# Half of the next tile's q projection moved ahead of the attention products on TensorE

## What is computed

```python
for i in range(6):
    x = attn_layer(shift_tokens(x), Wqkv[i], q_scale[i], k_scale[i], Wo[i]) + x
    x = ffn_layer(shift_tokens(x), ln_g[i], ln_b[i], W1[i], b1[i], W2[i], b2[i]) + x

def attn_layer(x, Wqkv, qs, ksc, Wo):      # 16 heads of 64
    q, k, v = split(x @ Wqkv)
    q, k = l2norm(q) * qs, l2norm(k) * ksc
    q, k = rotated(q), rotated(k)           # rotary tables with a scale
    # windows of 32 tokens: each sees itself and the window before, masked
    attn = softmax(where(mask, -inf, q @ k.T * 8))
    return (attn @ v) @ Wo
```

## Time and profile before

| | before |
|---|---|
| median of 3 runs | 3400.34 us (3400.24 to 3401.74) |
| the profiled execution's own time | 3401.79 us |
| its span, first to last instruction | 3400.0 us |
| mean granted TensorE clock, share of full speed | 0.993 |
| busy, TensorE matmuls | 3276.1 us (96%) |
| busy, TensorE weight loads | 2159.4 us (64%) |
| busy, VectorE | 2734.4 us (80%) |
| busy, ScalarE | 2226.2 us (65%) |
| busy, GpSimd | 2560.1 us (75%) |
| DMA | 52.53 MB, mean 15 GB/s |

### The profile page before, as it was taken

The page is one execution under the profiler, slowest core; times in us unless marked ns, Lnnn a source line. Parts: engine busy times, 40 slices in busy tenths (PEclk is TensorE's granted clock), DMA queues, the critical chain, the costliest instruction groups (busy, mean ns, idle before and its releaser), DMA issues. The chain is left out here.

```text
span 3400.0 us, 101399 instructions
## 1 busy us (share of the span) xinstructions
PE 3276.1 (96%) x42193; PEld 2159.4 (64%) x42193; DVE 2734.4 (80%) x3698; ACT 2226.2 (65%) x4397; POOL 2560.1 (75%) x2957
## 2 busy tenths in 40 slices
PE   8999699999999999999999999999999999999996
PEld 5555366666666666666666666666666666666664
DVE  2333598888988888888888888888888888988884
ACT  2222367777677676776776767767767667676774
POOL 0000498888888888888888888888888888888882
PEclk9999899999999999999999999999999999999999
DMA  2000001000001000001000010000010000000000
GB/s 73 1 1 1 4 11 36 11 11 8 11 17 36 8 11 11 11 17 34 11 11 8 11 42 11 8 11 11 11 41 9 11 11 8 16 13 18 11 11 13
DMA packets 62284, 52.53 MB, mean 15 GB/s; under 512 B 11526, under 2 KB 59396, under 8 KB 61828
## 3 DMA queue, kind: packets, MB, share of 16 engines
q1 hardware_dynamic: 61828, 46.05, 5.3%
HBM read 43.93 MB, written 2.10 MB: 14 GB/s over the span
## 5 line engine op out<-in xcount | busy, mean ns | idle before, releaser
L477 POOL TENSOR_TENSOR cosp<-cosp,sinp 128x1024 f32<-128x1024 f32 x384 | 905.7, 2370 | 33.9 <-DVE sinp L976 30.4
L584 PE MATMUL ps<-w_qk,xs 128*128 128x512 f32 x1536 | 748.1, 610 | 11.5 <-ACT sq L792 7.9
L688 PEld LDWEIGHTS ps<-px,w_vo 128*128 128x128 f32 x6144 | 702.5, 192 | 54.2 <-ACT px L833 33.6
L467 POOL TENSOR_TENSOR cosp<-cosp,rr 128x1024 f32<-128x1024 f32 x384 | 722.6, 1903 | 11.4
L688 PE MATMUL ps<-px,w_vo 128*128 128x128 f32 x6144 | 721.3, 276 | 1.9 <-ACT px L833 1.7
L973 DVE TENSOR_TENSOR cosp<-ps,tab 128x1024 f32<-128x1024 f32 x384 | 470.1, 1224 | 262.2 <-PE ps L584 255.8
L792 ACT ACTIVATE sq<-ps 128x1024 f32<-128x1024 f32 x384 | 392.9, 1023 | 344.3 <-DVE sinp L976 344.3
L737 PE MATMUL ps<-pT,xtm 32*128 32x512 f32 x3072 | 467.7, 624 | 34.3 <-DVE hh L1002 19.7
L584 PEld LDWEIGHTS ps<-w_qk,xs 128*128 128x128 f32 x1536 | 263.0, 191 | 343.6 <-issue 343.6
L976 DVE TENSOR_TENSOR sinp<-ps,tab 128x1024 f32<-128x1024 f32 x384 | 466.2, 1214 | 0.0
L982 DVE TENSOR_REDUCE ss<-sq 128x16 f32<-128x1024 f32 x384 | 455.5, 1186 | 3.1 <-POOL rr L452 1.8
(11 more groups left out here) (110 smaller groups left out, 4750.8 us busy)
## 6 DMA issues: line engine op xcount, KB each, us to landing
tab<-in_tab SPq DMA_DIRECT2D x96, 128.0 KB, 2.1
qks<-in_scales SPq DMA_DIRECT2D x96, 128.0 KB, 3.5
w_qk<-in_L_ffn_Wqkv SPq DMA_DIRECT2D x12, 512.0 KB, 6.1
w_v<-in_wv_t SPq DMA_DIRECT2D x6, 512.0 KB, 7.8
w_o<-in_L_ffn_Wo SPq DMA_DIRECT2D x6, 512.0 KB, 8.2
x<-in_L_attn_x SPq DMA_DIRECT2D x16, 128.0 KB, 5.3
out<-w_v SPq DMA_DIRECT2D x16, 128.0 KB, 2.5
w<-in_L_ffn_W SPq DMA_DIRECT2D x6, 341.0 KB
```

The source lines that it names most:

```text
L467: eng.tensor_tensor(v, v, rr[:, B % 2, HEADS * i:HEADS * i + HEADS].unsqueeze(2).to_broadcast([P, HEADS, DH]), ALU.mult).then_inc(rot_read ...
L477: eng.tensor_tensor(cosp[:, A % 2, i, :], cosp[:, A % 2, i, :], sinp[:, i, :], ALU.add).then_inc(rot_added, 1)
L584: t = eng.matmul(ps[:, u, :], xs[:, n % ROUND, :], w_qk[:, n // TILES % 2, i, 512 * u:512 * u + 512], start=True, stop=True)
L688: t = eng.matmul(Y, w_vo[:, E // TILES % 2, i // HP, i % HP, :], px[:, i, :], start=i == 0, stop=i == HEADS - 1)
```

## The change

The second half of `project(A, 0)` stays where it is, at the head of step A. Its first half (bank 0, the first 512 columns) is issued in the step before, between the scores of tile B and the products of tile C, with the three waits and the wait for the layer's weights. The first tile's half is issued ahead of the loop. `q_done` is still reported by the second half. No other engine's code changes.

```diff
             def project(n, i):
-                if n % TILES == 0:
-                    eng.wait_ge((wq_in, wk_in)[i], 16 * (n // TILES + 1))
-                for u in range(2):
+                if n % TILES == 0 and i == 1:
+                    eng.wait_ge(wk_in, 16 * (n // TILES + 1))
+                for u in range(i == 0, 2):
                     t = eng.matmul(ps[:, u, :], xs[:, n % ROUND, :], w_qk[:, n // TILES % 2, i, 512 * u:512 * u + 512], start=True, stop=True)
                 t.then_inc((q_done, k_done)[i], 1)
+
+            def project_start(n):
+                if n % TILES == 0:
+                    eng.wait_ge(wq_in, 16 * (n // TILES + 1))
+                eng.wait_ge(xs_ready, 2 * (n + 1))
+                after(eng, k_roped, 2 * n)
+                after(eng, sq_done, 2 * n)
+                eng.matmul(ps[:, 0, :], xs[:, n % ROUND, :], w_qk[:, n // TILES % 2, 0, 0:512], start=True, stop=True)
...
                 if tile(A):
-                    eng.wait_ge(xs_ready, 2 * (A + 1))
-                    after(eng, k_roped, 2 * A)
-                    after(eng, sq_done, 2 * A)
                     project(A, 0)
...
                     t.then_inc(sims_done, 1)
+                if tile(A + 1):
+                    project_start(A + 1)
                 if tile(C):
                     eng.wait_ge(p_turned, C + 1)
...
+            project_start(0)
             for s in range(LAST):
                 step(s)
```

## The result

The changed kernel takes **3496.0 us** (median of 4 runs, 3491.2 to 3499.2) against 3400.6 before (median of 4 runs): ratio **1.0278** (95% interval 1.0263 to 1.0293), 95 us slower. The forecast was 3463.6, 63 us slower, in a range from 3435 to 3492. The sign and the mechanism were right, two terms of the sum were too small, the forecast loss came out a third too small, and the median lies 4 us above the range.

A forecast was written before the change was run, and what follows sets the result against it. TensorE was taken to bound the kernel. Terms 71.8 + 8.6 - 11.1 - 6.0 gave +63.3 us, moving the median from 3400.3 to 3463.6 us; range some 3435 to 3480, about 3492 with the rival without gains.

The forecast's parts named there:

- What bounds the kernel: TensorE, busy 96% of the span, leads; VectorE waits 255.8 us for the projection, nearly all for k.
- The price of the hold: Behind the products, ScalarE's px copies hold Y until 1.75 us after them, in place of 1.93.
- Kinds 3 and 0: Steps with s mod 4 = 3 or 0: the half fills waits in the products; mean gains 0.27 and 0.15 us.
- with a fusion: 20 steps where a fusion of weights makes the turn of q late anyway: the whole 0.49 us gain counts.
- The gain from the half in kind 0: Steps with s mod 4 = 0: Y comes 0.15 us sooner, 40 steps, 6.0 us gained.
- Faster without a hold: Rival: px copies start before the products end, so Y follows at 1.07 us; total 3371 us, chance 0.08.
- No gain in kinds 3 and 0: Rival: VectorE's chain may lead in steps with s mod 4 = 3 or 0; +80 us, 3481, chance 0.20.
- The clock: Rival: idling before Y in half the steps lowers TensorE's clock; +158 us more, 3622, chance 0.02.
- The half projection itself: On TensorE, ahead of the products: 0.86 us plus 0.10 for an exposed weight load, 0.96 per half.
- Kinds 1 and 2: Steps with s mod 4 = 1 or 2, no wait to fill: +0.78 us each, 92 steps, +71.8 us.
- steps with an irregular stop: TensorE stops in the scores use up the wait in 11 steps, each losing 0.78 us: +8.6 us.
- late squares: Moved half waits for both squares of the tile before: cost 0, bound 0.1 us a step, 5 us up.

The follow-up runs named there:

- e3: Changed kernel with one of ScalarE's three px copies left out, zeros in its place: 3451.2 us, ratio 1.0139 to the kernel before.
- e1: Changed kernel with the half ahead of the products only in steps with s mod 4 = 3: 3395.2 us, ratio 0.9972 to the kernel before.
- e10: Changed kernel with the half ahead of the products only in steps with s mod 4 = 0: 3412.5 us, ratio 1.0035 to the kernel before.
- e4: Changed kernel with two of ScalarE's three px copies left out, zeros in their place: 3407.5 us, ratio 1.0014 to the kernel before.
- e6: Changed kernel with the whole projection of q ahead of the products in every step: 3639.3 us, ratio 1.0707 to the kernel before.
- e8: Changed kernel moving a half where s mod 4 = 3, a quarter where it is 0, otherwise nothing: 3383.1 us, ratio 0.9948 to the kernel before.

## Why the prediction was right and wrong

**What bounds the kernel** was right: TensorE leads before and after, and the waits of VectorE for k are nearly the same (255.8 and 252.9 us).

**The price of the hold** was right to 0.01 us: Y at 1.76 behind the products against 1.75 forecast, from the bare release in the earlier trace rows. Overlooked was that the transpose ahead of Y waits for the second copy. In the changed kernel it costs nothing of its own, since Y would be held anyway; in e3 it did.

**Kinds 3 and 0.** That the half fills kind 3's wait, and that POOL then limits the gain, was right, and e1 bears it out. The 0.47 against 0.46 with a fusion is in part luck: Y came 0.60 sooner there (2.67 to 2.07) and not 0.49, and the rest of the step grew by 0.13 and not 0.03. The gain from the half in kind 0 did not come: forecast was 0.15 a step, and e10's medians give a loss of 0.05.

**The rivals.** Faster without a hold: fallen, by the rows and by e4, where Y is free of the hold at 1.07 and the kernel, bound by POOL next, is still not faster than before. No gain in kinds 3 and 0: its mechanism has fallen, as VectorE still waits for k and e1 is 9 us faster, though its 3481 lies nearer to what was measured than the forecast. The clock: the granted clock is 0.994 on the mean, so the short idling ahead of Y in most steps does not lower it. The Trainium skill ("TensorE: Matmul & The Clock Gate", "A second HAM failure mode") would have it swing here; the trace does not agree, not even in e6, where TensorE idles 1.3 us in nearly every step and the clock is 0.993.

**The step that failed is the size of two terms.**

First, "The half projection itself": I took 0.10 for an exposed weight load, with bounds 0 and 0.2, and it is 0.20, a half of 1.06 and not 0.96: it adds two borders, one behind the scores and one ahead of the products, and each exposes 0.10. That is +0.10 in kinds 1 and 2 (92 steps, 9 us) and about as much in kind 0 (4 us).

Second, "Kinds 1 and 2": I took Y's start as all that the hold moves. Behind an idle stretch Y's first weight load is not hidden either, and everything behind comes 0.10 later again (3.67 against 3.57), in kinds 3, 1 and 2: 138 x 0.10 = 14 us. In e4, where nothing holds Y, its load starts 0.09 ahead of its matmul and the 0.10 is gone (3.58). No bound of the forecast held this term, though the bare release of the earlier trace rows has it: with all its 32 records that group is 3.84 us long, where the earlier trace rows has 3.74.

```profile
3355.85 3.84 PE L688 MATMUL ps<-px,w_vo 128*128 128x128 f32 x32 [1.66 <-ACT px L833]
```

The 3.67 that the table has before the change in steps with a fusion is another case: there Y stands behind the fusion's 64-row matmuls, with no idle stretch ahead of it, and the load shows at that border.

With the turn of q behind POOL in kind 0 a little later than taken (0.06 from turn to k), the two make some 29 of the 32 us that are missing. The remainder is in steps with an irregular stop, forecast at 8.6 us; by the medians of the table, 28 turns at 1.99 and 20 at 1.44 (kinds 3, 0, 1 and 2 added, without and with a fusion) are 85 us of the 95, so that some 10 are left. The steps off their median add 12.5 us to the medians before and 22.3 after, which is these 10. One such step, in e8 in kind 3, where the stop has used up the wait and the half then costs like in kinds 1 and 2:

```profile
2015.76 0.31 PE L738 MATMUL ps<-kT,qT 64*32 64x64 f32 x6 [2.04 <-issue]
2015.99 1.13 PE L600 MATMUL ps<-w_qk,xs 128*128 128x512 f32 x2
2017.05 2.00 PE L753 MATMUL ps<-pT,xtm 32*128 32x512 f32 x16
2018.98 1.13 PE L587 MATMUL ps<-w_qk,xs 128*128 128x512 f32 x2
2020.34 0.30 PE L692 MATMUL ps<-ident,xs 128*128 128x128 f32 x1 [0.23 <-ACT px L849]
```

The range did add the bounds that point the same way, but its ends are not quite their sums. Downward 10, 14 and 10 us from 3463.6 give 3430 and not 3435. Upward 3492 is the rival without gains (3481) with the 10 us of borders and without the 5 of late squares. What put the measured time outside is the term that had no bound at all, the 14 us of Y's first load.

## What to carry to other kernels

Before work is moved out of a stretch, ask what it hid there: here the projection of q covered ScalarE's copies by 0.17 us only, and taking half of it away won 0.17 and cost 1.06. Filling a wait pays in the steps that have one, and only with a piece that leaves the wait's other effect in place: a quarter in one kind of step and a half in another made the kernel 18 us faster, the same half everywhere 95 us slower. Price a split matmul with an exposed weight load at each border it adds, and one more for the first instruction behind an idle stretch (here 0.10 us each).

## What was not expected of the hardware

- A border between full-array float32 matmuls and those on 32 or 64 rows exposed 0.10 us of weight load in either direction, while full-array matmuls in a row hid it (half a projection: 1.06 against 0.86 us).
- The first weight load behind an idle stretch showed in what follows: 3.67 us for Y instead of 3.57.
- TensorE's stops inside the scores, for which the profile shows no releaser, are not a constant of the kernel: 22.4 us in 22 before, 23.6 in 24 after, and 37.0 in 26 where a wait for a square was put right ahead of the scores.
